# Two gated cross-attention layers on one core: the per-token chain of the first layer spread over two loop bodies, and one scaling of the second layer put behind two low parts

## The chip, the cores and the metric

The kernel runs on 1 core of a Trainium2 chip. The metric is the device time of one execution in microseconds. A core has five engines that matter here, each with its own instruction stream, in program order: TensorE (PE; matmul, with PEld for its weight loads), VectorE (DVE), ScalarE (ACT), GpSimd (POOL), and SyncE (SP), which only issues DMAs here. They meet at semaphores.

## What is computed

x is 16 batches of 256 tokens of 256 features; the context has the same shape. Four residual blocks follow one another, each on the layer-normalised x, each gated by a tanh:

```
x = x + tanh(g_xattn[0]) * L0_xattn(layernorm(x), ctx)   # 16 heads of 64, causal, softmax
x = x + tanh(g_ffn[0])   * L0_ffn(layernorm(x))
x = x + tanh(g_xattn[1]) * L1_xattn(layernorm(x), ctx)   # 16 heads of 16
x = x + tanh(g_ffn[1])   * L1_ffn(layernorm(x))          # a shared MLP and one of two routed ones

# L0_ffn, per token, no token sees another:
h   = gamma1 * rms(x)
q   = h @ Wq + bq
k,v = split((h @ Wdown + bdown) @ Wup + bup)             # 16 heads of 16 within one token
att = softmax over g of (q[h] . k[g]) / 4                # 16 x 16 per token
x   = x + (att @ v) @ Wo + bo
h2  = gamma2 * rms(x)
x   = x + sum over 8 experts e of softmax(h2 @ Wg + bg)[e] * (h2 @ We[e])
```

## The kernel before

The 16 batches go through the first layer one after the other, then through the second, with the end of the first beside the start of the second. In the first layer three batches are under way in one loop body: body(a, b, c, nxt) does the attention of batch a, the first half of L0_ffn ("mix") of batch b = a - 1, and the second half ("moe", the experts) of batch c = a - 2, and it prepares the projections of nxt = a + 1. A body has 20 steps, s = 0 to 19, a head of the attention each for 16 of them; every engine has its own function `body` with the same steps, and the order in it is written out by hand. So what stands late in one engine's step delays all that stands behind it on that engine, and through the semaphores other engines.

The tables mix_at, expert_at, add_at, score_at and gather_at (lines 221 to 226) say at which step which piece of mix and moe stands. In the kernel before, TensorE transposes h at step 2 and makes q, down, up0 and up1 at steps 3 to 6. GpSimd multiplies query by key in four pieces (line 371: two token halves t, two head halves u, 128 x 2048 elements each) into the two halves of the buffer prod; VectorE sums each (line 655, steps 7, 9, 11, 12), makes the softmax (lines 662 to 672, steps 12 and 13); GpSimd weighs the values in four pieces (weigh, line 385); VectorE sums them (mix_gather, line 678, steps 15, 16, 18, 19). Each piece of GpSimd waits until the sum of two pieces before has emptied its half of prod. At the begin of the next body TensorE transposes the result o ("oT"), ScalarE and VectorE make its high and low parts, TensorE makes "out" (fo), and VectorE adds bias and residual (moe_residual, lines 685 and 688), takes squares (moe_squares, step 1), scales by r2 (moe_normalise, line 706, step 2). Then follow the transposes of h2 and the gate (steps 4 and 5), and the experts.

Every body of VectorE begins with the low part of oT, the variance of x1 (lines 587 to 592), the residual, mix_normalise (lines 621 to 627, with n in line 623), and then the maximum of the first head (line 745). mix_rms (line 633) makes h at step 0, and line 772 copies x1 to x1res at step 1. pre_normalise (line 601) makes the next batch's xn at step 7. GpSimd's `power` (line 337) makes each of the inverse roots. At the end of a body VectorE takes the attention's result (attn_final, lines 757 and 761), behind gather 3 in its order; TensorE's part of it is attn_out (line 980).

The small banks of PSUM for mix and moe ("side") are two, used in turns in the order of a list (line 232). The second layer has bodies of its own: at the begin of each, VectorE finishes the MLP's result of the batch before (ffn_sum, line 1516, and the scaling of ffn_final, line 1523) and makes the low parts of the transposed tokens xfT and x0T (line 1437), whose high parts ScalarE casts (line 1313).

Of the kernel before, what the change touches and what calls it, by code (L numbers as in the profile page):

```python
# [20 lines left out]
B, S, D = 16, 256, 256  # L21
P = 128
# [9 lines left out]
E = 8  # L32
# [134 lines left out]
def layer0(nc, ins, x2, left, right, both):  # L167
# [14 lines left out]
    xin, ctxin, xn = sb(left, "xin", [P, NT, D]), sb(left, "ctxin", [P, ND, S]), sb(left, "xn", [P, NT, D])  # L182
# [6 lines left out]
    oT = qT  # L189
# [11 lines left out]
    x1res, n, h = sb(right, "x1res", [P, NT, D]), sb(right, "n", [P, NT, D]), sb(right, "h", [P, NT, D])  # L201
# [7 lines left out]
    o, foT = h, hT  # L209
# [6 lines left out]
    for s in range(STEPS):  # L216
# [4 lines left out]
    mix_at = {2: "hT", 3: "q", 4: "down", 5: "up0", 6: "up1"}  # L221
    expert_at = {6: 0, 7: 1, 8: 2, 10: 3, 12: 4, 14: 5, 15: 6, 17: 7}
    add_at = {7: 0, 8: 1, 9: 2, 10: 3, 12: 4, 14: 5, 15: 6, 17: 7}
    score_at = {7: 0, 9: 1, 11: 2, 12: 3}

    gather_at = {15: 0, 16: 1, 18: 2, 19: 3}
# [5 lines left out]
                     ["oT", "out", "hT", "q", "down", "h2T", "up0", "gate", "up1"] + [f"we{j}" for j in range(E)] + ["idle"])  # L232
# [38 lines left out]
    def sync(sp):  # L271
        def load(b):
            if not first(b):
                sp.wait_ge(xn_ready, b)
# [40 lines left out]
        yield 17  # L315
# [6 lines left out]
    def gpsimd(pool):  # L322
# [66 lines left out]
        def body(a, b, c, nxt):  # L389
            yield BEGIN  # L390
            if a is not None:
                mask(a)
            if b is not None:
                power(varB_ready, rstdB_ready, varB, rstdB, b)
            if b is not None:
                power(ms1_ready, r1_ready, ms1, r1, b)
            if c is not None:
                power(ms2_ready, r2_ready, ms2, r2, c)
            if nxt is not None:
                split_context(nxt)  # L400
                power(varA_ready, rstdA_ready, varA, rstdA, nxt)
            if b is not None:
                yield 5.5
                query_key(b, 0, 0)
                yield 6.5
                query_key(b, 0, 1)
                yield 8.5
                query_key(b, 1, 0)
                yield 9.5
# [6 lines left out]
        power(varA_ready, rstdA_ready, varA, rstdA, 0)  # L416
        run(body(0, None, None, 1))
# [12 lines left out]
    def scalar(act):  # L430
# [68 lines left out]
        def before_exp(b, c, s):  # L499
# [7 lines left out]
            if c is not None and s == 4:  # L507
                high(side, "h2T", c, h2T[0], h2T_hi, gamma2)

        def beside_head(a, b, c, nxt, s):  # L510

            if c is not None and s == 5:
# [4 lines left out]
            if c is not None and s == 6:  # L517
# [18 lines left out]
        def body(a, b, c, nxt):  # L536
            yield BEGIN
            if c is not None:
                high(side, "oT", c, foT[0], foT_hi)
# [39 lines left out]
    def vector(dve):  # L579
# [101 lines left out]
        def moe_residual(c):  # L681
# [6 lines left out]
            V.tensor_tensor(y[:], y[:], n[:], ALU.add)  # L688
# [1217 lines left out]
```

## Time and profile before

| | us |
|---|---|
| median of 3 runs | 2502.35 |
| the runs | 2502.28 to 2506.46 |
| the profiled execution | 2502.84 |
| its span, first to last instruction | 2501.0 |

| engine | busy us | share of the span |
|---|---|---|
| PE | 2227.4 | 89% |
| PEld | 1887.5 | 75% |
| DVE | 1480.4 | 59% |
| ACT | 1267.7 | 51% |
| POOL | 1023.1 | 41% |

Durations are read from the profiled execution. A row of the timeline gives the start in us from the span's start, the duration of the instruction (or of several alike in a row, with their count as xN), and in brackets how long the engine was idle before it and what ended that. Matmuls are pipelined: their durations overlap, and it is their starts that count.

### The profile page before, as it was taken

How to read it: one execution, taken by the hardware profiler on the slowest of the kernel's cores; microseconds unless marked ns; L12 is line 12 of the kernel's file. 1: busy time of each engine (PE TensorE's matmuls, PEld its weight loads, DVE VectorE, ACT ScalarE, POOL GpSimd, SP SyncE). 2: the span in 40 equal slices, each digit the busy share in tenths (PEclk: the TensorE clock that was granted, in tenths of full speed). 3: DMA queues.
4: the chain of work that ended last, by engine and by line, in shares of the span. 5: the costliest groups of instructions: out<-in, count | busy, mean ns of one | idle time of the engine just before them, and what ended most of it. 6: DMA issues, size and time to landing. Idle time of an engine off the chain costs nothing.

```text
span 2501.0 us, 47888 instructions
## 1 busy us (share of the span) xinstructions
PE 2227.4 (89%) x16000; PEld 1887.5 (75%) x16000; DVE 1480.4 (59%) x3922; ACT 1267.7 (51%) x3969; POOL 1023.1 (41%) x907
## 2 busy tenths in 40 slices
PE   5888899898888888888875799999999999999998
PEld 4667677777777777777664688888888888888888
DVE  4466666767667676676767635555555555555551
ACT  5655655556555565555633434455544444445541
POOL 1255555565555655556446213333332322333320
PEclk9999999999999999999977799999999999999999
DMA  4000000000000000000110200000000000000000
GB/s 154 8 12 14 6 17 17 17 13 4 17 17 17 13 4 17 17 17 4 39 32 13 110 16 7 13 17 17 17 17 17 17 17 16 5 13 17 17 9 9
DMA packets 26000, 51.40 MB, mean 21 GB/s; under 512 B 6160, under 2 KB 7312, under 8 KB 24784
## 3 DMA queue, kind: packets, MB, share of 16 engines
q1 hardware_dynamic: 25936, 50.57, 6.0%
q8 instruction: 37, 0.61, 0.1%
q14 instruction: 27, 0.22, 0.0%
HBM read 42.17 MB, written 8.39 MB: 20 GB/s over the span
## 4 chain that ended last, share of the span: by engine, by line
PE 57%; DVE 15%; ACT 8%; POOL 6%; issue 6%; DVEq 4%; POOLq 2%; DMA 0%; ACTq 0%
PE l_ffn L1714 13%; POOL l_prod L385 5%; PE l_ffn L161 4%; PE l_attn L161 4%; PE l_ffn L162 4%; PE l_ffn L163 4%; PE l_attn L1675 4%; PE l_attn L163 3%; PE l_attn L162 3%; DVEq L735 3%; PE l_side L161 3%; PE l_heads L1689 2%; POOLq L355 2%; PE l_side L163 2%; PE l_side L162 2%
## 5 line engine op out<-in xcount | busy, mean ns | idle before, releaser
L1253 POOL TENSOR_SCALAR l_probs<-l_probs,l_rinv 128x256 f32<-128x256 f32 x512 | 240.3, 484 | 479.2 <-DVE l_rinv L1492 478.3
L1376 ACT ACTIVATE l_probs<-l_score,l_negmax 128x256 f32<-128x256 f32 x512 | 239.1, 474 | 268.2 <-DVE l_negmax L1487 268.1
L385 POOL TENSOR_TENSOR l_prod<-l_att,l_kv 128x2048 f32<-128x2048 f32 x64 | 288.5, 4542 | 164.6 <-DVE l_att L672 164.6
L371 POOL TENSOR_TENSOR l_prod<-l_q,l_kv 128x2048 f32<-128x2048 f32 x64 | 291.2, 4561 | 150.7 <-DVE l_att L655 86.6
L1714 PE MATMUL l_ffn<-l_w,l_hid 128*128 128x256 f32 x1536 | 348.6, 381 | 1.0 <-ACT l_hid L1337 1.0
L1714 PEld LDWEIGHTS l_ffn<-l_w,l_hid 128*128 128x128 f32 x1536 | 286.2, 190 | 48.8 <-issue 12.7
L1499 DVE COPY l_probsT<-l_attn 128x512 f32<-128x512 f32 x240 | 164.5, 686 | 142.8 <-PE l_attn L1675 142.8
L745 DVE CUSTOM_DVE_ANT_0 l_probs<-l_score,l_mbias 128x256 f32<-128x256 f32 (+1 forms) x512 | 161.3, 352 | 144.9 <-PE l_score L947 95.8
L678 DVE TENSOR_REDUCE l_h<-l_prod 128x128 f32<-128x2048 f32 x64 | 146.3, 2286 | 107.5 <-POOL l_prod L385 107.2
L468 ACT ACTIVATE l_probs<-l_probs,l_negmax 128x256 f32<-128x256 f32 x256 | 130.8, 511 | 107.7 <-DVE l_negmax L745 106.6
L1487 DVE TENSOR_REDUCE l_negmax<-l_score 128x2 f32<-128x512 f32 x256 | 175.0, 684 | 15.0 <-PE l_score L1663 13.7
L485 ACT COPY l_probsT<-l_attn 128x384 f32<-128x384 f32 x256 | 120.9, 472 | 112.8 <-PE l_attn L957 112.7
L1337 ACT ACTIVATE l_hid<-l_ffn,l_b 128x256 f32<-128x256 f32 x384 | 162.1, 482 | 19.4 <-PE l_ffn L163 18.1
L1675 PE MATMUL l_attn<-l_ident,l_probs 128*128 128x128 f32 x1024 | 157.1, 279 | 11.4 <-DVE l_probsT L1499 6.6
L161 PE MATMUL l_side<-l_we_hi,l_h2T_hi 128*128 128x256 f32 x512 | 159.8, 312 | 2.2 <-DVE l_acc L729 1.8
L161 PE MATMUL l_attn<-l_cT_hi,l_wk_hi 128*128 128x256 f32 x384 | 124.0, 323 | 40.6 <-DVE l_xT_lo L609 39.0
L655 DVE TENSOR_REDUCE l_att<-l_prod 128x128 f32<-128x2048 f32 x64 | 145.8, 2279 | 5.0 <-issue 4.4
L162 PE MATMUL l_side<-l_we_lo,l_h2T_hi 128*128 128x256 f32 x512 | 147.5, 288 | 0.0
L163 PE MATMUL l_side<-l_we_hi,l_h2T_lo 128*128 128x256 f32 x512 | 147.1, 287 | 0.0
L476 ACT ACTIVATE l_probs<-l_probs,l_rinv 128x256 f32<-128x256 f32 x256 | 127.6, 498 | 24.3 <-DVE l_rinv L751 24.3
L1675 PEld LDWEIGHTS l_attn<-l_ident,l_probs 128*128 128x128 f32 x1024 | 118.8, 143 | 25.4 <-issue 12.4
L1238 POOL TENSOR_TENSOR l_rstdF<-l_varF,l_neghalf 128x2 f32<-128x2 f32 x16 | 11.2, 701 | 303.1 <-DVE l_varF L1421 303.1
(261 smaller groups left out, 7177.2 us busy)
## 6 DMA issues: line engine op xcount, KB each, us to landing
l_ctxin<-in_ctx SPq DMA_DIRECT2D x32, 256.0 KB, 3.0
l_xin<-in_x SPq DMA_DIRECT2D x16, 256.0 KB, 2.6
l_x<-in_x SPq DMA_DIRECT2D x16, 256.0 KB, 2.6
x<-l_acc SPq DMA_DIRECT2D x16, 256.0 KB, 2.0
l_xin<-x SPq DMA_DIRECT2D x16, 256.0 KB, 3.1
l_x<-x SPq DMA_DIRECT2D x16, 256.0 KB, 2.6
out<-l_x SPq DMA_DIRECT2D x16, 256.0 KB, 2.0
l_hid<-in_w SPq DMA_DIRECT2D x2, 1536.0 KB, 8.2
```

Source lines behind the costliest of these rows:

```text
L161: last = nc.tensor.matmul(out, wh, xh, start=n == 0, stop=False)
L162: last = nc.tensor.matmul(out, wh, xl, start=False, stop=False)
L163: last = nc.tensor.matmul(out, wl, xh, start=False, stop=n == len(terms) - 1)
L371: nc.gpsimd.tensor_tensor(prod[:, u].rearrange("p (h g d) -> p h g d", h=half, g=H), q4[:, u * half:(u + 1) * half].unsqueeze(2).to_broadc ...
L385: nc.gpsimd.tensor_tensor(prod[:, u].rearrange("p (h d g) -> p h d g", h=half, d=HD), a4.unsqueeze(2).to_broadcast([P, half, HD, H]), v4.u ...
L1253: last = nc.gpsimd.tensor_scalar(probs[:, j % 4, t * S:(t + 1) * S], probs[:, j % 4, t * S:(t + 1) * S], rinv[:, j, t:t + 1], 1.0, ALU.mul ...
L1337: last = nc.scalar.activation(hid[:, c, :], ps[:, u * S:(u + 1) * S], ACT.Relu, bias=b1[:, c:c + 1])
L1376: last = nc.scalar.activation(probs[:, s % 4, t * S:(t + 1) * S], ps[:, t * S:(t + 1) * S], ACT.Exp, bias=negmax[:, s, t:t + 1], accum_out ...
L1487: V.tensor_reduce(negmax[:, j], ps[:].rearrange("p (t k) -> p t k", t=NT), axis=AX.X, op=ALU.max, negate=True).then_inc(max_ready, 1)
L1499: V.tensor_copy(probsT[:, j % RING, :], ps[:]).then_inc(free, 1)
L1675: last = T.transpose(ps[:, kt * S + t * P:kt * S + (t + 1) * P], probs[:, j % 4, t * S + kt * P:t * S + (kt + 1) * P], ident[:])
L1714: last = T.matmul(ps[:, 0:D], hid[:, c, t * P:(t + 1) * P], w2[:, c, :], start=c == 0, stop=c == 3 * NHC - 1)
```

## The change

In the first layer the pieces of mix and moe stand at other steps. mix starts one step later. The third and fourth weighing go to the begin of the next body on GpSimd (the fourth behind the inverse root r1), their gathers to the begin and to step 2 of the next body on VectorE. oT, out, h2T and gate go from the begin and steps 4 and 5 to steps 3, 4, 7 and 8; the experts stand at steps 9 to 18 in place of 6 to 17. GpSimd builds the mask of the next batch at the end of a body and not its own at the begin. Since n of the batch c is needed after n of the batch b is written, VectorE copies it to a new buffer nres, at step 9 beside the copy to x1res. For room, xn now lies in xin, o in y and foT in h2T; so the load of the next x waits for the cast of its transposes. In the second layer ffn_final's sum stays in its place, and its scaling goes behind the low parts of xfT and x0T.

```diff
-    xin, ctxin, xn = sb(left, "xin", [P, NT, D]), sb(left, "ctxin", [P, ND, S]), sb(left, "xn", [P, NT, D])
+    xin, ctxin = sb(left, "xin", [P, NT, D]), sb(left, "ctxin", [P, ND, S])
...
-    oT = qT
+    xn, oT = xin, qT
...
-    o, foT = h, hT
+    o, foT = y, h2T
...
-    mix_at = {2: "hT", 3: "q", 4: "down", 5: "up0", 6: "up1"}
-    expert_at = {6: 0, 7: 1, 8: 2, 10: 3, 12: 4, 14: 5, 15: 6, 17: 7}
-    add_at = {7: 0, 8: 1, 9: 2, 10: 3, 12: 4, 14: 5, 15: 6, 17: 7}
-    score_at = {7: 0, 9: 1, 11: 2, 12: 3}
-    gather_at = {15: 0, 16: 1, 18: 2, 19: 3}
+    mix_at = {3: "hT", 4: "q", 5: "down", 6: "up0", 7: "up1"}
+    moe_at = {3: "oT", 4: "out", 7: "h2T", 8: "gate"}
+    expert_at = {9: 0, 10: 1, 11: 2, 13: 3, 14: 4, 16: 5, 17: 6, 18: 7}
+    add_at = {10: 0, 11: 1, 12: 2, 14: 3, 15: 4, 17: 5, 18: 6, 19: 7}
+    score_at = {8: 0, 9: 1, 11: 2, 12: 3}
+    gather_at = {16: 0, 18: 1}
...
-                     ["oT", "out", "hT", "q", "down", "h2T", "up0", "gate", "up1"] + [f"we{j}" for j in range(E)] + ["idle"])
+                     ["hT", "oT", "q", "out", "down", "up0", "up1", "h2T", "gate"] + [f"we{j}" for j in range(E)] + ["idle"])
...
-                sp.wait_ge(xn_ready, b)
+                sp.wait_ge(xT_hi, b)
...
# GpSimd, body
-            if a is not None:
-                mask(a)
+            if c is not None:
+                weigh(c, 2)
             if b is not None:
                 power(varB_ready, rstdB_ready, varB, rstdB, b)
-            if b is not None:
                 power(ms1_ready, r1_ready, ms1, r1, b)
+            yield 0.5
             if c is not None:
-                power(ms2_ready, r2_ready, ms2, r2, c)
+                weigh(c, 3)
+            yield 3.2
             if nxt is not None:
                 split_context(nxt)
                 power(varA_ready, rstdA_ready, varA, rstdA, nxt)
+            yield 5.2
+            if c is not None:
+                power(ms2_ready, r2_ready, ms2, r2, c)
             if b is not None:
-                yield 5.5
+                yield 6.5
                 query_key(b, 0, 0)
...
-                for piece in range(4):
-                    yield 13.5 + piece
-                    weigh(b, piece)
+                yield 13.8
+                weigh(b, 0)
+                yield 15
+                weigh(b, 1)
+            yield 15.9
+            if nxt is not None:
+                mask(nxt)
...
# VectorE
-            V.tensor_tensor(y[:], y[:], n[:], ALU.add)
+            V.tensor_tensor(y[:], y[:], nres[:], ALU.add)
...
-            if s == 0 and b is not None:
+            if s == 1 and b is not None:
                 mix_rms(b)
-            if s == 1:
-                if c is not None:
-                    moe_squares(c)
-                if b is not None:
-                    V.tensor_copy(x1res[:], x1[:]).then_inc(x1_copied, 1)
+            if s == 2 and c is not None:
+                mix_gather(c, 3)
...
             if c is not None:
-                if s == 2:
+                use = moe_at.get(s)
+                if use == "oT":
+                    low(side, "oT", c, foT, foT_hi)
+                elif use == "out":
+                    moe_residual(c)
+                elif s == 5:
+                    moe_squares(c)
+                elif s == 6:
                     moe_normalise(c)
...
+            if s == 9 and b is not None:
+                V.tensor_copy(nres[:], n[:])
+                V.tensor_copy(x1res[:], x1[:]).then_inc(x1_copied, 1)
             if nxt is not None:
-                if s == 3:
+                if s == 4:
                     pre_variance(nxt)
-                elif s == 7:
+                elif s == 8:
                     pre_normalise(nxt)
...
             yield BEGIN
-            if c is not None:
-                low(side, "oT", c, foT, foT_hi)
             if b is not None:
                 dve.drain()
                 variance(x1, statB, mvB, varB, varB_ready)
             yield BEGIN_OUT
             if c is not None:
-                moe_residual(c)
+                mix_gather(c, 2)
             if b is not None:
                 mix_normalise(b)
...
# TensorE: oT and out go from the begin of the body to steps 3 and 4, h2T and gate to 7 and 8
# second layer, VectorE
         def ffn_final(b):
-            ffn_sum(b, 1)
-            dve.drain()
             dve.wait_ge(x3_copied, b + 1)
...
             if c is not None:
-                ffn_final(c)
+                ffn_sum(c, 1)
             if b is not None and not first(b):
                 begin(b)
+            if c is not None:
+                ffn_final(c)
```

## Rows read from the trace of the kernel before

**Rows 1.** Windows: length, busy (count) of PE, PEld, DVE, ACT, POOL, granted clock, DMA, GB/s

```profile
608.00:686.40 78.40, 68.71 (x488) 56.99 (x488) 54.57 (x155) 45.49 (x144) 42.54 (x17) 0.98 0.04 14
...
680.00:684.00 4.00, 4.00 (x21) 3.48 (x21) 2.69 (x6) 2.27 (x8) 1.03 (x1) 0.57 0.00 0
```

**Rows 2.** One line's instructions: min/median/max ns, first and last start

```profile
L761 DVE SCALAR_TENSOR_TENSOR l_x<-l_ytmp,l_tg,l_x x16: 751/752/756, 95.8 to 1267.2; 128x512 f32<-128x512 f32 x16
```

**Rows 3.** Chain of waits around a seam of bodies: start, us, what

```profile
635.35 0.65 PE l_side L879 x4
...
640.30 0.69 DVE l_y L685
...
643.32 0.42 DVE l_probs L745
```

**Rows 4.** Waits of PE in one body, 608 to 686.4: total, times, longest

```profile
PE l_attn L161 <- DVE l_xT_lo L609: 2.5, 1, 2.5
PE l_side L879 <- DVE l_h L678: 1.5, 1, 1.5
```

**Rows 5.** Timeline of PE: attn_out, then the start of one expert and what follows

```profile
626.75 7.07 PE L980 MATMUL l_attn<-l_wo,l_qT 128*128 128x256 f32 x32
...
662.15 0.39 PE L161 MATMUL l_side<-l_we_hi,l_h2T_hi 128*128 128x256 f32 x1
...
663.67 0.27 PE L955 MATMUL l_attn<-l_ident,l_probs 128*128 128x128 f32 x1
```

**Rows 6.** Timeline of DVE from the softmax of one body into the next

```profile
614.07 0.69 DVE L672 TENSOR_TENSOR l_att<-l_att,l_asum 128x512 f32<-128x512 f32 x1
...
635.12 0.68 DVE L757 TENSOR_TENSOR l_ytmp<-l_attn,l_bo 128x512 f32<-128x512 f32 x1
...
638.59 0.17 DVE L592 TENSOR_SCALAR l_varB<-l_mvB 128x2 f32<-128x2 f32 x1
...
641.93 0.73 DVE L623 TENSOR_SCALAR l_n<-l_x,l_mvB,l_rstdB 128x256 f32<-128x256 f32 x2
...
643.94 0.61 DVE L633 TENSOR_SCALAR l_h<-l_n,l_r 128x256 f32<-128x256 f32 x2
...
656.79 0.67 DVE L651 TENSOR_TENSOR l_kv<-l_side,l_bup 128x512 f32<-128x512 f32 x1
...
667.64 0.74 DVE L601 TENSOR_SCALAR l_xn<-l_xin,l_mvA,l_rstdA 128x256 f32<-128x256 f32 x2
668.29 2.28 DVE L655 TENSOR_REDUCE l_att<-l_prod 128x128 f32<-128x2048 f32 x1
```

**Rows 7.** Timeline of POOL in the same stretch

```profile
614.84 18.03 POOL L385 TENSOR_TENSOR l_prod<-l_att,l_kv 128x2048 f32<-128x2048 f32 x4 [12.18 <-DVE l_att L672]
...
643.22 0.69 POOL L337 TENSOR_TENSOR l_r<-l_ms,l_neghalf 128x2 f32<-128x2 f32 x1 [3.68 <-DVE l_ms L627]
...
657.54 9.10 POOL L371 TENSOR_TENSOR l_prod<-l_q,l_kv 128x2048 f32<-128x2048 f32 x2 [3.93 <-DVE l_kv L651]
```

**Rows 8.** Timelines of POOL and DVE in two other places, early and at the layers' seam

```profile
113.74 9.03 POOL L371 TENSOR_TENSOR l_prod<-l_q,l_kv 128x2048 f32<-128x2048 f32 x2 [3.33 <-DVE l_kv L651]
119.28 3.97 DVE L601 TENSOR_SCALAR l_xn<-l_xin,l_mvA,l_rstdA 128x256 f32<-128x256 f32 x2
...
1353.11 4.54 POOL L385 TENSOR_TENSOR l_prod<-l_att,l_kv 128x2048 f32<-128x2048 f32 x1
1355.69 2.51 DVE L1481 SCALAR_TENSOR_TENSOR l_q<-l_qhi,l_again,l_qfull 128x512 fp32r<-128x512 f32 x1 [1.08 <-ACT l_qhi L1328]
```

**Rows 9.** Timelines of PE and DVE at the end of the first layer's last body

```profile
1253.39 8.83 PE L980 MATMUL l_attn<-l_wo,l_qT 128*128 128x256 f32 x32 [0.73 <-ACT l_qT L534]
...
1266.42 0.68 DVE L757 TENSOR_TENSOR l_ytmp<-l_attn,l_bo 128x512 f32<-128x512 f32 x1
```

**Rows 10.** Timelines of DVE and ACT at a seam of second-layer bodies

```profile
1834.56 0.75 DVE L1523 SCALAR_TENSOR_TENSOR l_x<-l_x,l_tg,l_x3res 128x512 f32<-128x512 f32 x1 [0.16 <-issue]
...
1835.14 0.59 ACT L1313 CAST l_x0T_hi<-l_ffn 128x512 fp32r<-128x512 f32 x1
...
1835.83 0.68 DVE L1437 TENSOR_TENSOR l_x0T_lo<-l_ffn,l_x0T_hi 128x512 fp32r<-128x512 f32 x1
```

More of the change, by code:

```diff
@@ L200, in layer0 @@
     x1, ytmp = sb(right, "x1", [P, NT, D]), sb(right, "ytmp", [P, NT, D])
-    x1res, n, h = sb(right, "x1res", [P, NT, D]), sb(right, "n", [P, NT, D]), sb(right, "h", [P, NT, D])
+    x1res, nres, n, h = sb(right, "x1res", [P, NT, D]), sb(right, "nres", [P, NT, D]), sb(right, "n", [P, NT, D]), sb(right, "h", [P, NT, D])
     statB, mvB, varB, rstdB = sb(right, "statB", [P, NT, 6]), sb(right, "mvB", [P, NT, 2]), sb(right, "varB", [P, NT]), sb(right, "rstdB", [P, NT])
@@ L314, in sync @@
         load_residual(B - 1)
-        yield 17
+        yield 19.6
         store(B - 3)
@@ L506, in before_exp @@
                 nc.scalar.activation(dT[0][:], ps[0:LAT, 0:S], ACT.Identity, bias=bdown[:]).then_inc(dT_hi, 1)
-            if c is not None and s == 4:
+            if c is not None and moe_at.get(s) == "oT":
+                high(side, "oT", c, foT[0], foT_hi)
+            if c is not None and moe_at.get(s) == "h2T":
                 high(side, "h2T", c, h2T[0], h2T_hi, gamma2)
         def beside_head(a, b, c, nxt, s):
-            if c is not None and s == 5:
+            if c is not None and s == 8:
                 act.wait_ge(glog_ready, c + 1)
@@ L516, in beside_head @@
                 last.then_inc(gexp_done, 1)
-            if c is not None and s == 6:
+            if c is not None and s == 9:
                 act.wait_ge(gsum_ready, c + 1)
@@ L783, in beside_head @@
             if c is not None:
-                if s == 2:
+                use = moe_at.get(s)
[6 more added lines that the diff above has]
+                elif s == 6:
                     moe_normalise(c)
-                elif s == 4:
+                elif use == "h2T":
                     low(side, "h2T", c, h2T, h2T_hi, gamma2)
-                elif s == 5:
+                elif use == "gate":
                     moe_gate_logits(c)
-                elif s == 6:
+                elif s == 9:
                     moe_gate(c)
@@ L823, in body @@
             yield BEGIN
-            if c is not None:
-                low(side, "oT", c, foT, foT_hi)
             if b is not None:
@@ L1011, in beside_head @@
             if c is not None:
-                if s == 4:
+                use = moe_at.get(s)
+                if use == "oT":
+                    pe.wait_ge(gathered, 4 * (c + 1))
+                    transpose4(side, "oT", c, o)
+                elif use == "out":
+                    side.emptied(pe, "oT", c)
+                    tokens(side, "out", c, foT, fo, D)
+                elif use == "h2T":
                     pe.wait_ge(h2_ready, c + 1)
                     transpose4(side, "h2T", c, y)
-                elif s == 5:
+                elif use == "gate":
                     side.emptied(pe, "h2T", c)
@@ L1022, in body @@
             yield BEGIN
-            if c is not None:
-                pe.wait_ge(gathered, 4 * (c + 1))
-                transpose4(side, "oT", c, o)
             if a is not None:
@@ L1030, in body @@
             yield BEGIN_OUT
-            if c is not None:
-                side.emptied(pe, "oT", c)
-                tokens(side, "out", c, foT, fo, D)
             if a is not None:
@@ L1616, in vector @@
         run(body(None, B - 1, B - 2, None))
+        ffn_sum(B - 1, 1)
+        dve.drain()
         ffn_final(B - 1)
```

8 lines of the change are left out of this document (4 added, 4 removed).

## The prediction, made before the changed kernel was built or run

> **What bounds the kernel now.** First I read the window of one steady body of the first layer and a stretch of four us in it [rows 1]: in 78.40 us TensorE is busy 68.71, VectorE 54.57, GpSimd 42.54. TensorE is the fullest engine, yet idle for 9.7 us of a body, and for about 4 us of it the clock is 0.57, between its two levels of 1.2 and 2.4 GHz. The spacing of the 16 copies of line 761, (1267.2 - 95.8) / 15 = 78.1 us, says that this body repeats [rows 2]. Then the chain of waits around the seam of two bodies [rows 3]: the last gather ends in the transposes of the mixed tokens (635.35), their product and the residual sum (640.30), and only then comes the first maximum of the next body (643.32). The wait table of TensorE names the two largest stalls of a body [rows 4]: 2.5 us for the low part of xT and 1.5 us for the last gather. So the layer is bound by a loop over engines that runs in program order on each: GpSimd products, VectorE sums, TensorE, VectorE. It is not bound by one engine, and a change of order can cost as easily as it can bring.
>
> I count time t from the end of attn_out on TensorE, 626.75 + 7.07 = 633.82 [rows 5]; the next one ends at t = 78.4. Marks of the kernel before: first maximum at 9.5 (643.32); first half of kv stored at 23.6 (656.79 + 0.67); first score sum stored at 36.8 (668.29 + 2.28); attention weights ready at 59.3 (614.07 + 0.69, one body on) [rows 3, 6].
>
> **The change part by part, first layer.** Removed at the seam: line 757 waits no longer for gathers 2 and 3; it started at t = 1.3 and can start at 0.1. The low part of oT (0.69 and its gap, about 0.8) goes from between line 761 and the variance. From the end of the variance (638.59 + 0.17) to the scaling of line 623 (641.93) 3.2 us pass; one tiny product stays, so 3.1 us of waiting for "out" and of residual (2 x 0.69) go, and gather 2 comes in (2.3, a sum over 2048 elements like line 655). The first maximum stands at 9.5 - 1.2 - 0.8 - 3.1 + 2.4 = 6.8, so 2.7 us are won here [rows 3, 6].
>
> Added behind it: GpSimd makes r1 (0.69, then at 6.7) and at once starts the fourth weighing, a quarter of the 18.03 us for four, 4.5 us: t = 7.4 to 12.0 [rows 7]. VectorE asks for line 633 at 8.6 (after two maxima and a reciprocal that waits for ScalarE). That is a scaling from SBUF to SBUF. What such a one does beside a GpSimd product the trace shows twice [rows 8]: at 119.28 the two scalings of line 601 took 3.97 us in place of 0.74, because two products filled 113.74 to 122.77, and they ended when those did; at 1355.69 line 1481 (two SBUF inputs) took 2.51 us and ended 0.5 behind the product that ran from 1353.11 to 1357.65. VectorE stands still, with all that is queued behind. So line 633 ends at 12.6, gather 3 (2.29, behind one more maximum) at 15.6, and oT's transposes start at 15.7, where TensorE has waited 2.5 us.
> The Trainium skill, "SBUF — State Buffer", section "Who interferes with whom", says that a VectorE instruction in a two-port mode or with two SBUF inputs and a GpSimd instruction exclude each other for a whole instruction, whichever starts first. The trace agrees with it in both rows above; by a rule of shared bandwidth line 633 would cost some tenths instead of 3.4 us and the result would be the first rival below.
>
> From oT on, in program order: TensorE does oT (0.45), q2, a pair of scores, q and out. A group of twelve matmuls takes 1.52 (662.15 to 663.67) [rows 5], a pair of scores with its gap 0.95: out ends at 21.6. VectorE: residual 1.55, variance 1.3, a maximum with reciprocal 0.8, the low part of "down" 0.5, squares 1.75, another 0.8, first half of kv 0.67: 28.7 against 23.6 before.
>
> Here is the second collision. GpSimd starts the first query-key product 0.08 after that store (656.79 + 0.67 to 657.54) [rows 6, 7], and moe_normalise (line 706, two scalings SBUF to SBUF) is now the next thing of VectorE. The first of the two slips in, the second waits for the product, 4.55 us. h2 is ready at 33.5; without the collision at 29.3. TensorE waits for it about 5 us. Then h2T 0.45, head transpose 0.42, values 0.8, scores 0.85, gate and its sum 1.9 bring VectorE to line 601 at 38.4; line 601 takes 0.74 and the first score sum 2.28: 41.4 against 36.8.
>
> Third: the two copies (x1res moved from step 1, nres added, about 0.42 each) stand a maximum and two reciprocals behind that sum, and GpSimd has begun its next product 0.08 behind it: they wait from 42.2 to 45.8. With copies 0.8 and the second sum 2.29: 48.9. From there the order is like before: maxima 0.75 each (four), three expert sums 0.95 each, a wait for xT's high part 2.1, two more score sums 2.3 each, softmax 1.5 and 1.9: 48.9 + 3.0 + 2.85 + 2.1 + 4.6 + 3.4 = 64.8; one maximum of the four lies beside the exponential, so 64 against 59.3. In the kernel before, 633.82 - 614.76 = 19.1 us follow until attn_out ends; now more experts stand late (steps 14, 16, 17, 18), one group of 1.52 more from there on, while some 0.4 of the waits there are filled: 20.2. The body ends at 84.2 in place of 78.4: **+5.8 us**. Hidden and taken as nothing: split of the context, mask (three instructions on GpSimd between weighings 1 and 2, which end before t = 84), xin's load (now from the end of its cast; the loads land with 20 us in hand), the store one or two steps later.
>
> Bounds. Below, no collision costs anything: 3.4, 4.2 and 3.6 us less on VectorE. TensorE's groups then bind: its 68.7 us busy now, less 1.6 for half-clocked matmuls, plus 8.4 of waits that stay (0.7, 0.6, 0.7 and 1.2 for oT in the first steps, 0.9 and 2.0 around the third expert, 1.7 for head copies, 0.6 at the end): 75.5, -2.9 per body. Above: the clock. After TensorE's wait of 2.5 us for xT, 680 to 684 ran at 0.57 [rows 1, 4], and twelve matmuls took about 2.6 in place of 1.4, some 1.6 us for a spell. The changed body has three waits of 2.5 to 5 us (oT, h2T, the third expert), so up to two spells more than now, +3.3: 87.5, or +9.1. I take +5.8, with the collisions whole, since the nearest rows show them whole, and the clock spells as hidden behind VectorE.
>
> **Ends of the first layer.** Body 1 has no batch in its moe part: only the third collision, +1 (0 to +4). The bodies from 2 to 15 have it all: 14 x 5.8 = +81. At the end, line 757 started at 1266.42 though attn_out had ended at 1253.39 + 8.83 = 1262.22 [rows 9]; with two gathers gone from before it, -4. Two weighings of the last batch leave the first body of the second layer, where they held up its head scalings on GpSimd: -9, against two steps more until the last x2 (+4) and the same collisions twice (+8). Together for the seam of the layers -1, between -12 and +10.
>
> **Second layer.** It looks as if 0.75 us went from before two low parts, 14 times. But in the row of line 1437 x0T's low part starts at 1835.83 and ScalarE ends x0T's high part at 1835.14 + 0.59 = 1835.73 [rows 10]: the transposes and the cast set it, not the scaling at 1834.56. Gain at most 0.07 x 14 = -1. The scaling itself now stands before the first maximum, which comes 0.6 us later; that maximum's batch is next needed by TensorE at step 2, several us on, so I cost it at nothing (if the cover were gone: 0.6 x 14 = 8 us). The store is issued 1.3 us later and nothing waits for it in the body.
>
> **Sum.** 2502.84 (profiled execution; the span is 2501.0) + 81 + 1 - 1 - 1 = 2583; the median shown is 0.5 lower, so **2582 us**. Its own range, by 4.5 to 8 us per body and the seam's bounds: 2555 to 2625.
>
> **The rivals.**
> 1. The collisions don't bite: GpSimd yields, or VectorE's scalings come first. For it: line 601 in the steady body is untouched, 0.74 at 667.64, since it stands in a gap of GpSimd [rows 6, 7]. Against it: rows 8. Then -2.9 x 14 = -41, seam -9, -1: about 2452.
> 2. Half: line 633 waits (it must, as r1 and the fourth weighing come from GpSimd back to back), but line 706 gets both its scalings in before the product takes hold. That is a race of under 0.1 us. The body is then 77.5 to 79, -0.9 to +0.6: 2478 to 2505, middle 2490. It also needs line 601 to fall into the seam of two products.
> 3. The clock too, as in the upper bound: +9.1 x 14 = +127: 2632.
> The point from which slower decides: the seam gives 2.7 us and later stalls up to 4; more than about 3 us per body of collisions turns the sign.
>
> **How the numbers follow.** Forecast 0.49, rival 3 0.12, rival 2 0.22, rival 1 0.17. A difference of 0.2% (5 us) is what can be told from none. Faster: rival 1 whole and 0.16 of rival 2 = 0.33; within 0.2%: 0.05 (most of the rest of rival 2); slower: 0.49, 0.12 and the last 0.01 of rival 2 = 0.62. The range takes the forecast's own, most of rival 2 and the nearer half of rival 3: 2472 to 2630.
>
> **What would show it.** In the trace after: line 633 or line 706 at over 3 us in some bodies, and line 772 likewise; a TensorE wait for h2T of 4 to 5 us and for oT of 2 to 3; the wait for the last gather at the seam gone; line 761's spacing near 84. I am wrong if lines 633, 706 and 772 keep 0.35 and 0.42 (rival 1), or if only 633 is long and the spacing is 77.5 to 79 (rival 2). If the second layer gets shorter by 10 us, the cast was not what set x0T.

## The result: 2661.6 us, slower by 6.3%

| | before | after |
|---|---|---|
| median of 4 runs each, us | 2504.4 | 2661.62 |
| the runs, us | 2502.28 to 2507.33 | 2660.12 to 2665.72 |
| ratio of the times, 95% interval | | 1.063, 1.0611 to 1.0648 |
| span of the profiled execution, us | 2501.0 | 2660.8 |
| one steady body of the first layer, us | 78.4 | 88.68 |

The sign was forecast and so were the places; the size was not. The time after lies above the range (2472 to 2630), and the growth of 157 us is twice the forecast 80. One execution of all that follow stands apart, 4192.7 us in the kernel that fills one wait of TensorE; its ratio is from the other three, 2667.3 to 2668.0.

The page of the kernel after, its busy times and the granted clock over its span:

```profile
PE 2269.9 (85%) x16000; PEld 1925.9 (72%) x16000; DVE 1661.0 (62%) x3938; ACT 1267.4 (48%) x3969; POOL 1022.5 (38%) x907
...
PEclk9989899988998899899877779999999999999999
```

GpSimd does the same work in the same time (1023 us), VectorE is busy 181 us longer with 16 instructions more (the copies to nres), and TensorE 42 us longer with the same 16000. An engine that is "busy" longer with the same work has been held up inside its instructions: VectorE at a shared resource, TensorE by its clock.

The windows of one steady body after and of four stretches in it; the columns are those of [rows 1]:

```profile
789.51:878.19 88.68, 71.77 (x490) 59.80 (x490) 65.78 (x156) 45.41 (x142) 42.59 (x17) 0.92 0.04 12
...
804.62:808.62 4.00, 4.00 (x22) 3.41 (x21) 1.47 (x3) 3.00 (x9) 0.00 (x0) 0.57 0.00 0
820.62:824.62 4.00, 1.02 (x5) 1.02 (x6) 4.00 (x7) 0.00 (x0) 4.00 (x2) 0.67 0.00 0
824.62:828.62 4.00, 4.00 (x22) 2.57 (x20) 1.04 (x4) 2.92 (x9) 3.31 (x1) 0.50 0.00 0
840.62:844.62 4.00, 2.32 (x11) 2.32 (x12) 2.64 (x12) 2.15 (x7) 3.69 (x1) 0.73 0.09 33
```

A granted clock of 0.50 is the level of 1.2 GHz for the whole stretch, 1.00 that of 2.4 GHz. Twice the missing part of the clock, times the length, is the time spent at the lower level: summed over a body's windows of 4 us, 3.4 us before and 13.6 us after. VectorE has 65.8 us of work in the body where it had 54.6 [rows 1].

Attention's last scaling line 761 has become line 771, and the others of VectorE are 10 lines further down as well (633 is 643, 706 is 716, 601 is 611, 757 is 767, 745 is 755, 651 is 661, 655 is 665, 678 is 688). The row that answers to [rows 2], and those of the three expected collisions, min/median/max in ns:

```profile
L771 DVE SCALAR_TENSOR_TENSOR l_x<-l_ytmp,l_tg,l_x x16: 750/752/753, 95.1 to 1410.0; 128x512 f32<-128x512 f32 x16
...
L643 DVE TENSOR_SCALAR l_h<-l_n,l_r x32: 332/694/3611, 101.3 to 1426.8; 128x256 f32<-128x256 f32 x32
...
L716 DVE TENSOR_SCALAR l_y<-l_y,l_r x32: 343/350/4594, 197.8 to 1542.6; 128x256 f32<-128x256 f32 x32
...
L809 DVE COPY l_nres<-l_n x16: 419/4348/4401, 128.1 to 1464.4; 128x512 f32<-128x512 f32 x16
```

The 14 bodies between the second and the last x1 take 88.65 us each, (1410.1 - 169.0) / 14, where they took 78.76. The difference of the two spans, 159.8 us, is made of: the first x1 -0.8; the next body +5.1 (73.8 for 68.7); 14 bodies x 9.9 = +138.5; everything behind the last x1 +17.0.

TensorE's waits in the same body, which answer to [rows 4] (us in total, times, longest):

```profile
PE l_side L894 <- DVE l_y L716: 5.4, 1, 5.4
PE l_side L161 <- DVE l_acc L739: 4.5, 1, 4.5
PE l_side L894 <- DVE l_y L688: 2.1, 1, 2.1
...
PE l_side L894 <- DVE l_h L643: 1.1, 1, 1.1
```

The wait at the body's begin for the last gather is gone, as it should; in its place stand h2, the third expert, oT and h. VectorE's and GpSimd's timelines of the body, to be laid beside [rows 6] and [rows 7] (TensorE's attn_out before it ended at 781.50 + 7.07 = 788.57, which is t = 0):

```profile
781.50 7.07 PE L995 MATMUL l_attn<-l_wo,l_qT 128*128 128x256 f32 x32
```
```profile
795.26 0.42 DVE L755 CUSTOM_DVE_ANT_0 l_probs<-l_score,l_mbias 128x256 f32<-128x256 f32 x1 [0.18 <-issue]
...
797.04 4.08 DVE L643 TENSOR_SCALAR l_h<-l_n,l_r 128x256 f32<-128x256 f32 x2
801.67 2.26 DVE L688 TENSOR_REDUCE l_y<-l_prod 128x128 f32<-128x2048 f32 x1
811.56 0.69 DVE L695 TENSOR_TENSOR l_y<-l_side,l_bfo 128x512 f32<-128x512 f32 x1 [0.75 <-PE l_side L163]
...
818.14 0.67 DVE L661 TENSOR_TENSOR l_kv<-l_side,l_bup 128x512 f32<-128x512 f32 x1
818.73 4.82 DVE L716 TENSOR_SCALAR l_y<-l_y,l_r 128x256 f32<-128x256 f32 x2
...
830.44 0.73 DVE L611 TENSOR_SCALAR l_xin<-l_xin,l_mvA,l_rstdA 128x256 f32<-128x256 f32 x2
831.08 2.28 DVE L665 TENSOR_REDUCE l_att<-l_prod 128x128 f32<-128x2048 f32 x1
833.97 4.35 DVE L809 COPY l_nres<-l_n 128x512 f32<-128x512 f32 x1
838.57 2.27 DVE L665 TENSOR_REDUCE l_att<-l_prod 128x128 f32<-128x2048 f32 x1
...
856.67 0.69 DVE L682 TENSOR_TENSOR l_att<-l_att,l_asum 128x512 f32<-128x512 f32 x1
862.06 2.29 DVE L688 TENSOR_REDUCE l_y<-l_prod 128x128 f32<-128x2048 f32 x1 [0.17 <-POOL l_prod L386]
```
```profile
795.81 4.55 POOL L386 TENSOR_TENSOR l_prod<-l_att,l_kv 128x2048 f32<-128x2048 f32 x1
...
818.90 9.03 POOL L372 TENSOR_TENSOR l_prod<-l_q,l_kv 128x2048 f32<-128x2048 f32 x2 [0.72 <-DVE l_kv L661]
833.44 4.59 POOL L372 TENSOR_TENSOR l_prod<-l_q,l_kv 128x2048 f32<-128x2048 f32 x1 [5.51 <-DVE l_att L665]
...
857.44 9.18 POOL L386 TENSOR_TENSOR l_prod<-l_att,l_kv 128x2048 f32<-128x2048 f32 x2 [11.98 <-DVE l_att L682]
```

Each long row of VectorE begins inside a product of GpSimd and ends 0.2 to 0.8 us behind its end (801.12 for 800.36; 838.32 for 838.03), or behind the first of two (823.55; the two begin at 818.90). Each stands where the forecast put it. The gather at 862.06 is the contrast: a sum over one SBUF tile, 2.29 us beside a product, not held up.

Behind the last x1, VectorE's and GpSimd's rows at the first norm of the second layer's MLP:

```profile
1512.18 9.02 DVE L1461 TENSOR_SCALAR l_xf<-l_x,l_mvF,l_rstdF 128x256 f32<-128x256 f32 x2 [0.82 <-POOL l_rstdF L1254]
```
```profile
1512.11 8.93 POOL L386 TENSOR_TENSOR l_prod<-l_att,l_kv 128x2048 f32<-128x2048 f32 x2
```

Two scalings of 0.41 us each took 4.5 us each, one behind each of the last batch's two moved weighings. From this norm to the next one 126.0 us pass; it was 110.1.

### The profile page after: what moved, and what is told of

Same layout as the page of the kernel before. It is cut to its first block, busy times and chain, and to the rows that moved or that the text cites. A ratio compares the mean times of both kernels' runs of the same rounds, so it can differ in the third digit from the quotient of the medians.

```text
span 2660.8 us, 47926 instructions
## 1 busy us (share of the span) xinstructions
PE 2269.9 (85%) x16000; PEld 1925.9 (72%) x16000; DVE 1661.0 (62%) x3938; ACT 1267.4 (48%) x3969; POOL 1022.5 (38%) x907
## 4 chain that ended last, share of the span: by engine, by line
PE 60%; DVE 21%; issue 9%; ACT 4%; DVEq 3%; POOL 1%; DMA 1%; ACTq 0%; SPq 0%; POOLq 0%
PE l_ffn L1732 13%; PE l_attn L995 4%; PE l_ffn L161 4%; PE l_ffn L162 3%; PE l_ffn L163 3%; PE l_attn L1693 3%; PE l_attn L161 3%; PE l_side L161 3%; DVE l_y L688 3%; DVE l_att L665 3%; PE l_attn L163 3%; PE l_attn L162 3%; DVE l_y L716 2%; PE l_heads L1707 2%; PE l_side L162 2%
## 5 line engine op out<-in xcount | busy, mean ns | idle before, releaser
L161 PE MATMUL l_side<-l_we_hi,l_h2T_hi 128*128 128x256 f32 x512 | 165.8, 324 | 57.2 <-DVE l_acc L739 57.0
L161 PEld LDWEIGHTS l_side<-l_we_hi,l_h2T_hi 128*128 128x128 f32 x512 | 106.1, 207 | 71.2 <-DVE l_acc L739 66.2
L163 PE MATMUL l_side<-l_we_hi,l_h2T_lo 128*128 128x256 f32 x512 | 154.0, 301 | 0.0
L162 PE MATMUL l_side<-l_we_lo,l_h2T_hi 128*128 128x256 f32 x512 | 154.0, 301 | 0.0
L688 DVE TENSOR_REDUCE l_y<-l_prod 128x128 f32<-128x2048 f32 x64 | 145.9, 2279 | 12.3 <-POOL l_prod L386 12.1
L894 PE MATMUL l_side<-l_ident,l_y 128*128 128x128 f32 x128 | 29.9, 377 | 125.3 <-DVE l_y L716 75.7
L161 PE MATMUL l_attn<-l_xT_hi,l_wq_hi 128*128 128x256 f32 x384 | 123.1, 320 | 9.0 <-DVE l_k_lo L1480 5.1
```

Source lines behind the costliest of these rows:

```text
L161: last = nc.tensor.matmul(out, wh, xh, start=n == 0, stop=False)
L162: last = nc.tensor.matmul(out, wh, xl, start=False, stop=False)
L163: last = nc.tensor.matmul(out, wl, xh, start=False, stop=n == len(terms) - 1)
L688: V.tensor_reduce(o[:, t, u * P:(u + 1) * P], prod[:, u].rearrange("p (x g) -> p x g", g=H), axis=AX.X, op=ALU.add).then_inc(gathered, 1)
```

## The experiments

Each comes with its edit; the ratio is to the kernel before, of runs taken beside it, with the 95% interval. "Body" is a steady body of the first layer.

### The three collisions, one by one and together

```diff
# y1: GpSimd's fourth weighing waits for h
             yield 0.5
             if c is not None:
+                pool.wait_ge(h_ready, b + 1)   # where there is a b
                 weigh(c, 3)
# y2: the first query-key product waits for h2
                 yield 6.5
+                if c is not None:
+                    pool.wait_ge(h2_ready, c + 1)
                 query_key(b, 0, 0)
# y3: the copies go from step 9 to step 8, just ahead of the first score sum
-            if s == 9 and b is not None:
-                V.tensor_copy(nres[:], n[:])
-                V.tensor_copy(x1res[:], x1[:]).then_inc(x1_copied, 1)
...
+                if s == 8:
+                    V.tensor_copy(nres[:], n[:])
+                    V.tensor_copy(x1res[:], x1[:]).then_inc(x1_copied, 1)
                 if s in score_at:
```

y1, expected: 

> The changed kernel, but GpSimd's fourth weighing waits for h_ready, so VectorE's scaling to h (line 643) is not shut out for 3.5 us. The weighing and so gather 3 come about 2 us later, h's transposes 3 us earlier. Theory A (a collision stops VectorE for a whole product, and each long wait of TensorE is followed by a stretch at the half clock): gather 3 is what TensorE waits for next, so the end moves little: 0 to -1.5 us per body, 2640 to 2662 us. Rival B (collisions cost nothing, the new order of TensorE costs the time): 0 or slower, 2662 to 2690.

y2, expected: 

> The changed kernel, but GpSimd's first query-key product waits for h2_ready, so the second scaling of line 716 is not shut out. The products start 0.7 us later. Theory A: h2 is ready at 31 in place of 35, TensorE's wait for it falls from 5.4 to 1.5 us and the slow-clock stretch behind it (1.6 us) goes: -3.5 to -5.5 us per body, 14 bodies, 2585 to 2612 us, of the first layer 83.5 per body. Rival B: the products on the path start later, so 2662 to 2675. Rival C (the three collisions hide behind each other, each alone is worth little): -0 to -1.5 us per body, 2640 to 2662.

y3, expected: 

> The changed kernel, but the copies to nres and x1res stand just ahead of the first score sum, where GpSimd has finished two products and waits for that sum. Theory A: the copies take 0.4 us each and the second sum is stored 4 us earlier (its own product of 4.5 us then binds): -3 to -5 us per body, 15 bodies, 2587 to 2617 us. Rival B: no change, 2655 to 2668. Rival C: 2640 to 2662.

All three, expected: 

> The changed kernel with all three edits: no collision of the three is left. Theory A: 8 to 11 us less per body, 14 bodies and some for the first: 2505 to 2550 us, granted clock of the first layer back near 0.97. Rival B: near 2662. Rival C (they hide each other): the sum of the three single gains is much less than the gain of all three together.

In the last column h is the scaling of line 643, h2 that of line 716, xn that of line 611, and copy is line 809.

| | us | ratio | body, us | operations of VectorE over 2.5 us in a body |
|---|---|---|---|---|
| after | 2661.62 | 1.063 (1.0611 to 1.0648) | 88.65 | h 3.5, h2 4.6, copy 4.3 |
| y1 | 2668.88 | 1.0664 (1.0646 to 1.0683) | 88.8 | h2 4.6, copy 4.3 |
| y2 | 2642.54 | 1.0558 (1.0539 to 1.0577) | 87.1 to 88.5 | h 3.5, xn 4.7, copy 4.2 |
| y3 | 2630.88 | 1.0518 (1.0495 to 1.0541) | 84.4 and 89.7 in turns | h 3.5, h2 4.6 |
| all three | 2591.15 | 1.035 (1.0332 to 1.0368) | 83.3 to 83.9 | xn 4.7 |

None came out as theory A said: y1 is 7 us slower than the change, which is rival B's number there, though its body is as long as the change's; y2 gained 19 us where 50 to 76 were expected, y3 31 where 45 to 75 were, all three 70 where 112 to 157 were. Rival C had the size of y2, not that of y3, and it had that all three bring more than their single gains added up (70 for -7 + 19 + 31 = 43), yet not for its reason. The rows show why. In y2, the row of the scaling to h2 (line 718, min/median/max ns) is clean, and that of the scaling to xn (line 613), which was never held up in a steady body of the kernel after, is not:

```profile
L718 DVE TENSOR_SCALAR l_y<-l_y,l_r x32: 342/347/353, 200.8 to 1523.1; 128x256 f32<-128x256 f32 x32
...
L613 DVE TENSOR_SCALAR l_xin<-l_xin,l_mvA,l_rstdA x32: 392/425/4790, 14.7 to 1257.9; 128x256 f32<-128x256 f32 x32
```

VectorE comes earlier to xn, and now meets the second product. The product did not lose a victim, it took the next one in VectorE's order. In y1 nothing was won since the wait itself has a price. Counted from the body's first maximum, h is ready 3.5 us earlier, but gather 3, whose weighing now waits, ends 0.7 us later (9.4 for 8.7), and TensorE, which transposes h and then o, needs both: it waits 4.2 us for the gather, where it waited 1.1 for h and 2.1 for the gather. Its wait in y1:

```profile
PE l_side L895 <- DVE l_y L689: 4.2, 1, 4.2
```

In y3 the bodies are short and long in turns, with the same instructions. The windows of two in a row:

```profile
686.15:770.53 84.38, 70.97 (x490) 59.07 (x490) 61.84 (x156) 45.53 (x142) 42.60 (x17) 0.92 0.04 13
770.53:860.25 89.72, 76.11 (x490) 63.36 (x490) 61.87 (x156) 46.09 (x142) 42.52 (x17) 0.87 0.04 12
```

VectorE and GpSimd are busy equally long in each, and TensorE's long waits are the same (5.4, 2.1 and 1.1 us for h2, oT and h); what differs is the clock, 0.92 and 0.87, and the body by 5.3 us. What an edit on VectorE gave, the clock took back in every other body. No theory had that, and no run tells what makes the bodies differ in the first place.

One more edit to all three puts the scaling to xn ahead of the first half of kv:

```diff
+            if nxt is not None and s == 6:
+                pre_normalise(nxt)
             if b is not None and s in mix_at:
...
-                elif s == 8:
-                    pre_normalise(nxt)
```

> As the kernel with the three edits together (2591 us), and the scaling to xn also stands ahead of the first half of kv, since in that kernel it took 4.66 us behind the second product. Theory A (one collision gives place to the next, of the same 4 us): another 3 to 5 us per body, 14 bodies, 2520 to 2550 us. Rival C (TensorE's waits for the last gather and the half clock bind by now): 0 to -1 us per body, 2577 to 2591.

2591.44 us, ratio 1.0354 (1.0337 to 1.0371): nothing gained, so theory A missed again in the number and was borne out in kind. The rows of xn and of the two copies in it:

```profile
L614 DVE TENSOR_SCALAR l_xin<-l_xin,l_mvA,l_rstdA x32: 392/404/410, 14.0 to 1200.7; 128x256 f32<-128x256 f32 x32
...
L820 DVE COPY l_nres<-l_n x16: 417/2364/4677, 120.7 to 1387.9; 128x512 f32<-128x512 f32 x16
...
L821 DVE COPY l_x1res<-l_x x16: 409/416/4807, 122.6 to 1388.3; 128x512 f32<-128x512 f32 x16
```

xn is clean, and one of the two copies is held up in each of 15 bodies, in the first of them both (line 820 in nine, line 821 in seven): they stand at the place that y3 chose for them because GpSimd was idle there, and with xn out of the way VectorE is there before GpSimd is idle.

### No collision at all

```diff
# GpSimd: weighings 3 and 4 at the end of the body, the first product waits for h2
             if nxt is not None:
                 mask(nxt)
+            if b is not None:
+                yield 17
+                weigh(b, 2)
+                yield 18.5
+                weigh(b, 3)
...
+                if c is not None:
+                    pool.wait_ge(h2_ready, c + 1)
                 query_key(b, 0, 0)
# VectorE: gather 2 at step 19, gather 3 at the begin (was 2 at the begin, 3 at step 2); xn at step 6
# ScalarE, step 9, in place of VectorE
+            if b is not None and s == 9:
+                act.wait_ge(scored, 4 * b + 1)
+                nc.scalar.copy(nres[:], n[:])
+                nc.scalar.copy(x1res[:], x1[:]).then_inc(x1_copied, 1)
# VectorE waits for these copies (x1_copied) ahead of the residual sum
```

> The changed kernel with every meeting of GpSimd's long products and VectorE's copies and scalings taken away: the third and fourth weighing stand at the end of the body, gather 2 in the time in which VectorE waits for attn_out, gather 3 at the begin; the scaling to xn (line 611) stands ahead of the first half of kv; the two copies are ScalarE's; the first product waits for h2. Theory A (collisions, the ones that move in when one goes, and the slow clock behind TensorE's waits make the whole loss): 75 to 79 us per body of the first layer, 2470 to 2520 us in all, granted clock there 0.96 or more. Rival B (spreading the chain itself costs, by later experts and two more bodies of latency): still above 82 us per body, 2560 us or more.

2453.4 us, ratio 0.9804 (0.9788 to 0.9819): 8% less than the change and 2% less than the kernel before. The body of 75.1 us is in theory A's range, the time is 17 us below it. A steady body of it, and its row of query-key products:

```profile
769.62:844.71 75.09, 67.75 (x490) 56.66 (x490) 53.85 (x154) 46.17 (x144) 42.56 (x17) 0.98 0.05 14
```
```profile
796.06 18.16 POOL L372 TENSOR_TENSOR l_prod<-l_q,l_kv 128x2048 f32<-128x2048 f32 x4 [2.06 <-DVE l_y L723]
```

VectorE is busy 53.85 us in place of 65.78 in the same kind of body; the longest of its rows there is a sum of 2.29; and the four products run through without a pause, since each sum is done in time to empty its half. The copies on ScalarE (0.61 and 0.62 us at 806.67, inside those products) are not held up. The Trainium skill, "SBUF — State Buffer", section "Who interferes with whom", has it that ScalarE never waits for another engine there and that a sum has no mode in which it does; both agree with this row and with the gather at 862.06 above.

Two edits put one thing back each. First the copies, on VectorE at step 9:

> The kernel without collisions (2453 us, 75.1 us per body) with one put back: the two copies are VectorE's again and stand at step 9, as in the change, a maximum and two reciprocals behind the first score sum. Theory A: one collision costs a body what it cost in the kernel before, 4 to 5.5 us, its own 4.3 and something for the clock: 2510 to 2535 us. Rival (with two long waits less the body has room for one): 2453 to 2480.

2526.86 us, ratio 1.0114 (1.0079 to 1.0149), as theory A said: 73 us over 15 bodies, in each of which a copy is held up: 4.9 for each, more than its own 4.1 to 4.8. Second, the weighings and gathers where the change has them:

> The kernel without collisions (2453 us), with the third and fourth weighing and their gathers put back where the change has them: weighing 4 behind r1, beside line 643, and gather 3 at step 2. The other three edits stay. Theory A: line 643 takes 3.5 us again, TensorE waits some 2 us for h and oT together, kv's first half comes 4 to 5 us later and a slow-clock stretch returns: 79 to 82 us per body, 2510 to 2550 us. Rival (TensorE's own work binds the body and hides this one): 2455 to 2480.

2514.75 us, ratio 1.0046 (1.0033 to 1.0058), body 78.3: theory A's time, at its low edge, with a body just under its range. Line 643 takes 3.5 us again and TensorE waits 2.1 for oT and 1.1 for h. The norm at the seam of the layers is held up again too (125.9 us to the next one; without the weighings there 115.6). Together the two that were put back are 135 of the 208 us between the change and the kernel without collisions; the third, the second scaling of line 716, was not put back by itself.

### One collision in the kernel before

```diff
-                if b is not None:
-                    V.tensor_copy(x1res[:], x1[:]).then_inc(x1_copied, 1)
...
+            if s == 8 and b is not None:
+                V.tensor_copy(x1res[:], x1[:]).then_inc(x1_copied, 1)
```

> The kernel before with one edit: the copy to x1res (line 772) stands at step 8, a maximum and a reciprocal behind the first score sum, where GpSimd has just begun its third product. Theory A: it takes about 4 us in place of 0.4, and TensorE and VectorE, which have little room there, give 2 to 4 us of it to the body: 2530 to 2565 us. Rival (a single collision is hidden): 2500 to 2512.

2572.39 us, ratio 1.0275 (1.0259 to 1.0292). The row of the copy, and a body of that kernel:

```profile
L772 DVE COPY l_x1res<-l_x x16: 415/4352/4423, 126.8 to 1385.7; 128x512 f32<-128x512 f32 x16
```
```profile
836.05:919.55 83.50, 70.95 (x487) 59.05 (x487) 58.48 (x155) 45.02 (x142) 42.42 (x17) 0.94 0.04 13
```

A copy of 0.42 us, moved seven steps, makes the kernel 68 us slower, 4.6 us for each of 15 bodies, past the upper end of what I expected. The clock of the body goes from 0.98 to 0.94: again more than the hold-up itself.

### The clock, by matmuls that compute nothing

```diff
+        def idle_products(use, batch, count):
+            ps, _, free, turn = side.at(use, batch)
+            pe.wait_ge(free, turn)
+            for _ in range(count):
+                T.matmul(ps[:, 0:D], fo[0][:, 0, 0:P], fo[0][:, 1, :], start=True, stop=True)
...
+                    idle_products("h2T", c, 38)
                     pe.wait_ge(h2_ready, c + 1)
```

They write into a bank that real products fill afterwards, in time in which TensorE waits anyway.

> The changed kernel with 38 idle matmuls of 128 x 256 on TensorE, into the bank that the transposes of h2 take next, in the time in which it waits for h2 (5.4 us). All waits for other engines stay. Theory A (the stretch at the half clock behind that wait is 1.6 us of the body): no slow stretch behind h2's transposes, 1.0 to 2.5 us less per body, 2625 to 2648 us. Rival (VectorE hides the clock, as the forecast took it): within 5 us of 2661. If the idle matmuls come late or are too many: up to +1 us per body.

2667.66 us, ratio 1.0658 (1.0638 to 1.0679): the rival's number. Windows of it, behind the wait for oT, in the wait for h2 (filled) and behind that for the third expert:

```profile
805.40:809.40 4.00, 4.00 (x20) 3.60 (x20) 1.47 (x3) 3.12 (x9) 0.00 (x0) 0.50 0.00 0
...
825.40:829.40 4.00, 3.92 (x35) 3.27 (x35) 2.83 (x14) 3.23 (x10) 4.00 (x1) 1.00 0.00 0
...
841.40:845.40 4.00, 3.61 (x17) 3.28 (x19) 2.47 (x10) 1.68 (x8) 3.57 (x1) 0.50 0.00 0
845.40:849.40 4.00, 4.00 (x24) 3.13 (x26) 2.24 (x1) 2.96 (x9) 0.00 (x0) 0.68 0.00 0
```

The clock stays at 1.00 behind the filled wait, and the way from kv's first half to the first score sum is 2.2 us shorter; but the other two slow stretches are twice as long, so the half-clock time of a body is 13.7 us as before, only elsewhere. The run did not decide between the theories. So all four waits were filled, with 9, 16, 34 and 34 idle matmuls ahead of h, oT, h2 and the third expert (the last into a bank of the head transposes):

> The changed kernel with idle matmuls of 128 x 256 on TensorE in four waits: 9 ahead of h's transposes, 16 ahead of oT's, 34 ahead of h2's, 34 ahead of the third expert's. All waits for other engines stay, and so do the three collisions. In the run with one filled wait the half-clock time of a body stayed 13.7 us and only moved; the stretch from kv's first half to the first score sum got 2.2 us shorter, the two other slow stretches cost 1.0 and 1.3 us more. Theory A (half clock costs some 4.5 us of the body): granted clock of the first layer 0.97 or more and 3 to 6 us less per body, 2580 to 2620 us. Rival B (VectorE hides the clock): within 8 us of 2661.

2609.2 us, ratio 1.0425 (1.0402 to 1.0448). 52 us fewer than the change, by 93 more matmuls in each body. A body, and VectorE in it:

```profile
841.99:925.64 83.65, 78.10 (x583) 66.90 (x583) 65.80 (x156) 45.51 (x142) 42.83 (x17) 1.00 0.04 13
```
```profile
869.06 0.67 DVE L661 TENSOR_TENSOR l_kv<-l_side,l_bup 128x512 f32<-128x512 f32 x1
869.65 4.97 DVE L716 TENSOR_SCALAR l_y<-l_y,l_r 128x256 f32<-128x256 f32 x2
...
879.78 2.28 DVE L665 TENSOR_REDUCE l_att<-l_prod 128x128 f32<-128x2048 f32 x1
882.66 4.32 DVE L809 COPY l_nres<-l_n 128x512 f32<-128x512 f32 x1
887.24 2.28 DVE L665 TENSOR_REDUCE l_att<-l_prod 128x128 f32<-128x2048 f32 x1
...
904.13 0.69 DVE L682 TENSOR_TENSOR l_att<-l_att,l_asum 128x512 f32<-128x512 f32 x1
```

VectorE is as busy as in the change (65.80 for 65.78 us) and is held up three times as there, the clock is 1.00 for the whole body, and the body is 5.0 us shorter. That is the price of the half clock by itself, and theory A. For the whole kernel less is left: the profiled execution, 2600.3 us, is the fastest of the four (the others took 2607.5 to 2611.5), and in it the 14 bodies give 68 us back (83.8 each) while the parts ahead of them and behind them take 5.6 us more.

### The second layer's part alone

Its edit is the second-layer part of the change, on the kernel before.

> The kernel before with the second layer's part of the change alone: the scaling of ffn_final behind the low parts of xfT and x0T. Theory A (the cast and the transposes set x0T's low part, not the scaling): -1 to 0 us, 2499 to 2505. Rival B (0.75 us less ahead of two low parts, 14 times): -10, 2491 to 2495. Rival C (the scaling now delays the first maximum): +8.

2504.53 us, ratio 1.0004 (0.9993 to 1.0016): theory A; rival B's -10 and rival C's +8 are outside the interval.

## Why the prediction was right in kind and wrong in size

**The step that failed** is the last of the first-layer sum: the clock spells were taken "as hidden behind VectorE", 0 us, and carried only as the upper bound of 3.3 per body. With the clock at 1.00, in the body with four filled waits, the forecast's marks stand within 0.6 us; t counts from attn_out's end, 841.04 there:

| t, us | forecast | change, clock full | change |
|---|---|---|---|
| first maximum | 6.8 | 6.7 | 6.7 |
| kv, first half stored | 28.7 | 28.7 | 30.2 |
| first score sum stored | 41.4 | 41.0 | 44.8 |
| second score sum stored | 48.9 | 48.5 | 52.3 |
| attention weights ready | 64 | 63.8 | 68.8 |
| next attn_out ends | 84.2 | 83.6 | 88.7 |

So the program order, the three collisions and their sizes were right, and the clock cost 5.0 us per body. The sum missed by 79.6 us: 57 of them are the 14 bodies, which grew by 9.9 us each and not by 5.8, and the clock's 5.0 is all of that 4.1 and a little more; the other 22 are the ends, below. Why it isn't hidden: a wait of VectorE behind a product makes TensorE wait, TensorE then comes back at half clock, and what it makes at half clock (q and out; h2T and the gate; the experts) is just what VectorE waits for next. The forecast counted the spells against TensorE's total and not against this chain. The size was off too: 10.2 us more of half clock in a body than before, not two spells more of 1.6 us each of loss. The Trainium skill, "TensorE: Matmul & The Clock Gate", section "Terms", estimates the loss as half of the throttled time; for 13.6 us that would be 6.8. The trace has 5.0 for 13.6, and in y3 5.3 for some 10 more (clock 0.87 for 0.92), so between a little under two fifths and a little over half of it is on the path.

**The steps that held.** Line 643 was asked at t = 8.5 (forecast 8.6) and ended at 12.5 (12.6); gather 3 ended at 15.4 (15.6); oT and h cost TensorE 2.1 and 1.1 (2.5 together); line 716's first scaling slipped in and its second took 4.56 (4.55); TensorE waited 5.4 for h2 (about 5); line 611 was not held up (0.73); the copies were, by 3.9 us beyond their own 0.42 (3.6). The seam gain of 2.7 us came whole.

**Rivals.** The first (no collision) is refuted for the change, but its number describes the kernel without collisions: 2452 against 2453.4, body 75.5 against 75.1. That kernel places more than the change does, so it is a check of the size, not of the change, and that the totals agree so closely is in part luck: the rival had 10 us less at the ends, and the trace has more there and less in the bodies. The second (line 716 gets both in) needed the race of under 0.1 us to go the other way, and it never did in 14 bodies. The third (clock too) named the mechanism, with +9.1 per body where 9.9 came, and I gave it 0.12. Its 2632 is a slip: the forecast's 2582 and 14 x 3.3 = 46 make 2628.

**The ends.** The body with no moe batch cost +5.1 and not +1: the copies took 4.4 us there as well. That is close to what one collision costs in the kernel before (4.6) and without collisions (4.9), of which I had hidden most; that the copies alone make it is argued, for the scaling to xn is held up in this body in both kernels (3.6 before, 4.6 after) and the clock up to the second x1 went from 0.93 to 0.88. The seam of the layers with the second layer came to +17.0 and not -2. The gather's way out was right (from the last x1 to the first norm 101.2 us for 102.4), but the two late weighings were only credited with leaving the head scalings alone; that they now stand beside the MLP's first norm was not seen, and there they hold up two scalings for 8.2 us and cost 15.9 to the next norm. The kernel without collisions needs 115.6 there, and 125.9 again with the weighings and gathers alone put back, so 10 of these 16 us are theirs. The rest of the second layer is at 69.3 us a body, as before, and its own edit is worth nothing, as forecast.

**What stays open.** No run tells why filling one wait lengthened the slow stretches at the two others, nor why the stretch between the norms at the layers' seam stays 5.5 us longer than in the kernel before (115.6 for 110.1) once the weighings have left it. What the hold-up of line 716 costs by itself was measured only beside others (y2), where xn took its place.

## What to carry to other kernels

An operation of VectorE that can be shut out by a long GpSimd instruction is not a cost of 0.4 us that goes wherever there is room: list where each such operation and each long product stands in time, and look at the pair again after every edit, because taking one meeting away brings VectorE early to the next. Order such pairs by a semaphore, where nothing is waiting for the product (in y1 something was, and it brought nothing), or give the copy to ScalarE; a place where GpSimd "is idle anyway" holds only as long as nothing ahead of it gets faster. And where a change makes TensorE wait longer, price the half clock behind the wait on the chain that follows it, not on TensorE's total.

## What the runs showed of the hardware

- Two scalings of VectorE back to back can both be shut out, one by each of two products back to back (9.02 us for two of 0.41, at 1512.18): GpSimd gets its turn between them. In line 716 the first got in and the second took 4.56.
- A small operation is not safe. The add of 128x2 elements that gives varB, 0.17 us as a rule, took 4.28 us once, at the same seam, beside a product from 1411.74 to 1416.27:

```profile
1412.01 4.28 DVE L602 TENSOR_SCALAR l_varB<-l_mvB 128x2 f32<-128x2 f32 x1
```

- Two bodies with the same instructions and the same hold-ups can differ by 5.3 us, with waits that differ by under 0.5 us each and a clock of 0.92 and 0.87 (y3), in turns, six times over.
- Idle matmuls in TensorE's waits shortened the kernel by 52 us. In one wait only they moved the half-clock time (13.7 us a body, before and after), in all four they took it away.
